# Sandwich layer on one core: inner tiles of the feed-forward block turned by DMA exchange and VectorE, weight parts and final norms moved to ScalarE, new orders

## What is computed

```python
x = x + _layernorm(attention(_layernorm(x), w_qkv, w_dense))      # causal, softmax over keys
x = x + _layernorm(ffn(_layernorm(x), w1, s1, w3, s3, w2, s2))
# ffn: every linear first quantises its input per row and block of 128 columns (amax / 448 + 1e-12)
g = linear_dsv3(xf, w1, w1_scale); u = linear_dsv3(xf, w3, w3_scale)
y = linear_dsv3(silu(g) * u, w2, w2_scale)
```

## Time and profile before

| | before |
|---|---|
| median of 3 runs | 1162.52 us |
| the profiled execution, its own time | 1162.25 us |
| its span, first to last instruction | 1160.4 us |
| TensorE busy | 1136.9 us (98%), 5618 matmuls and transposes |
| VectorE busy | 841.9 us (73%) |
| GpSimd busy | 743.9 us (64%) |
| ScalarE busy | 605.6 us (52%) |
| mean granted TensorE clock | 0.997 |

### The profile page before, as it was taken

How to read it: one execution, slowest core, us unless ns; L and a number is a source line. 1 busy time by engine, 2 the same in 40 slices (tenths; PEclk the granted TensorE clock), 3 DMA queues, 4 the chain that set the end, 5 groups by cost and what they waited for, 6 DMA issues and landing times. The chain is left out here.

```text
span 1160.4 us, 17601 instructions
## 1 busy us (share of the span) xinstructions
PE 1136.9 (98%) x5618; PEld 953.6 (82%) x5618; DVE 841.9 (73%) x1935; ACT 605.6 (52%) x1300; POOL 743.9 (64%) x829
## 2 busy tenths in 40 slices
PE   9999999999999999999999999999999999999996
PEld 7888888888888888888888888888887788888884
DVE  5545445458898897988888988988668955666568
ACT  6532324247766676767667676766578621111111
POOL 7844456435864955956838649558855767677636
PEclk9999999999999999999999999999999999999998
DMA  6443454326476585484574765754220011110101
GB/s 220 136 167 151 186 206 189 146 91 205 126 222 206 162 258 178 136 284 137 190 246 130 228 205 160 252 184 157 90 73 2 1 55 55 56 49 5 54 0 72
DMA packets 122098, 164.45 MB, mean 142 GB/s; under 512 B 10400, under 2 KB 95904, under 8 KB 118688
## 3 DMA queue, kind: packets, MB, share of 16 engines
q1 hardware_dynamic: 122016, 163.44, 42.8%
HBM read 98.78 MB, written 64.62 MB: 141 GB/s over the span
## 5 line engine op out<-in xcount | busy, mean ns | idle before, releaser
L816 POOL TENSOR_SCALAR probs_long<-probs_long,rsum 128x896 f32<-128x896 f32 (+9 forms) x124 | 118.0, 954 | 69.3 <-DVE rsum L1285 68.9
L1070 ACT ACTIVATE probs_long<-probs_long,negmax 128x896 f32<-128x896 f32 (+9 forms) x124 | 121.5, 980 | 70.5 <-DVE negmax L1279 69.7
L816 POOL TENSOR_SCALAR probs_short<-probs_short,rsum 128x416 f32<-128x416 f32 (+15 forms) x128 | 85.1, 669 | 112.9 <-DVE rsum L1285 112.2
L1520 PE MATMUL psS<-kT_hi,qT_hi 128*128 128x256 f32 (+8 forms) x384 | 134.7, 351 | 0.3
L1520 PE MATMUL psS<-kT_lo,qT_hi 128*128 128x256 f32 (+8 forms) x384 | 128.3, 334 | 0.0
L1520 PE MATMUL psS<-kT_hi,qT_lo 128*128 128x256 f32 (+8 forms) x384 | 128.3, 334 | 0.0
L1664 PE MATMUL psOY<-wd_hi,oT_hi 128*128 128x512 f32 x256 | 107.2, 419 | 2.0 <-DVE oT_lo L1214 1.2
L757 POOL TENSOR_TENSOR qT_lo<-q_raw,qT_hi 128x512 fp32r<-128x512 f32 x64 | 86.6, 1357 | 33.4 <-ACT qT_hi L1054 31.0
L1664 PE MATMUL psOY<-wd_hi,oT_lo 128*128 128x512 f32 x256 | 100.7, 393 | 0.0
L1664 PE MATMUL psOY<-wd_lo,oT_hi 128*128 128x512 f32 x256 | 100.4, 392 | 0.0
L1649 PE MATMUL psOY<-pT_hi,v_hi 128*128 128x512 f32 x222 | 92.5, 417 | 4.2 <-DVE pT_lo L1214 4.2
(11 more groups left out here) (185 smaller groups left out, 3293.4 us busy)
## 6 DMA issues: line engine op xcount, KB each, us to landing
q_raw<-q_scr SPq DMA_DIRECT2D x64, 256.0 KB, 3.5
p_scr<-probs_long SPq DMA_DIRECT2D x24, 512.0 KB, 3.2
probs_long<-p_scr SPq DMA_DIRECT2D x96, 128.0 KB, 3.5
raw<-in_w_qk SPq DMA_DIRECT2D x10, 1024.0 KB, 5.6
p_scr<-probs_long SPq DMA_DIRECT2D x21, 448.0 KB, 3.0
probs_long<-p_scr SPq DMA_DIRECT2D x84, 112.0 KB, 3.0
q_scr<-cB SPq DMA_DIRECT2D x16, 512.0 KB, 2.6
q_scr<-cA SPq DMA_DIRECT2D x16, 512.0 KB, 2.9
```

Of the source, the lines that this page charges most:

```text
L816: nc.gpsimd.tensor_scalar(row, row, rsum[:, column(t, h)], 1.0, ALU.mult, ALU.mult).then_inc(p_ready, 1)
L1070: nc.scalar.activation(row, row, ACT.Exp, bias=negmax[:, column(t, h)], scale=-1.0, accum_out=lsum[:, column(t, h)]).then_inc(e_done, 1)
L1520: last = nc.tensor.matmul(dst, a, b, start=(start and k == 0), stop=(stop and k == len(terms) - 1), skip_group_check=resumed)
```

## The change

In words:

- Inner tiles 0 to 52 are no longer turned by TensorE. GpSimd writes the scaled tile into a ring of four (`hidden`), SyncE stores it to DRAM (`hidden_away(n)`), then fetches tile n-1 with its 32-row blocks exchanged in four DMAs of 32 KB (`hidden_back(n-1)`), and VectorE turns the blocks (`turn_hidden`). High and low part are made from SBUF instead of PSUM. Tiles 53, 54, 55 (LAST_TURNS = 3) stay with TensorE (`turn_last`).
- The down product runs four tiles behind gate and up instead of two (LAG = 4). So the list of chunk 0 has four "DN" items instead of six, and four stand behind the last gate and up product instead of two.
- High parts of the weights of chunks 2 to 6 are copied by ScalarE (`hi_of_piece`); GpSimd takes the low part one step later (`low_of_piece`). Loads of up and down weights are separate, the up weights' one placed in step 5 of a chunk between a store and the fetch behind it.
- The last norms, for seven of the eight row tiles, are made of a sum that comes with the last addition, a square with its sum and the normalisation on ScalarE, and root and offset on GpSimd (`finish`, `square_last`, `norm_last`, `add_last`).
- `swap_back` in attention fetches 14 of 16 blocks (the two outer corners stay where they are).
- The tables that shift the items are replaced for all engines, attention included.

The diff, cut:

```diff
-    ATTENTION += [("X", 1), ("GU", 0), *[("Y", T - 1, h) for h in range(HG)], ("A", T - 1), ("X", 2), ("GU", 1), ("TH", 0)]
+    ATTENTION += [("X", 1), ("GU", 0), *[("Y", T - 1, h) for h in range(HG)], ("A", T - 1), ("X", 2), ("GU", 1)]
     for n in range(2, NT):
-        ATTENTION += [("X", n + 1)] * (n + 1 < NT) + [("GU", n), ("DN", n - 2), ("TH", n - 1)]
+        ATTENTION += [("X", n + 1)] * (n + 1 < NT) + [("GU", n)]
+        if n >= LAG:
+            ATTENTION.append(("DN", n - LAG))
+        if n >= LAG - 1:
+            ATTENTION += [("TT", n - LAG + 1), ("TH", n - LAG + 1)]
...
+            def hidden_away(n, m):
+                sp.wait_ge(h_ready, n + 1)
+                sp.dma_start(h_scr[m % RING], hidden[:, m % RING, :]).then_inc(h_out[m % 2], 16)
+            def hidden_back(m, stored):
+                slot = m % RING
+                sp.wait_ge(h_out[m % 2], stored)
+                for c in range(HG):
+                    sp.dma_start(hidden[c * SPAN:(c + 1) * SPAN, slot, :].rearrange("q (a x) -> q a x", a=HG),
+                                 h_scr[slot, :, c * CW // HG:(c + 1) * CW // HG].rearrange("(a q) x -> q a x", a=HG)
+                                 ).then_inc(h_in[slot], 16)
...
+                for m in range(2 * NT):
+                    hidden_away((2 * NT) * r + NT + m, NT + m)
+                    if m % NT == KT + 1:
+                        load_up(2 * r + 3 + m // NT)
+                    if m % NT == NT - 1:
+                        load_down(2 * r + 3 + m // NT)
+                    hidden_back(NT + m - 1, (16 * NT) * r + 16 * ((NT + m - 1) // 2 + 1))
...
                 for i in range(NT):
-                    quantise_hidden(c * NT + i, i % 2)
+                    quantise_hidden(c * NT + i, (0 if slot == 0 else NT) + i)
...
-                            prepare(c + 1, 1 - slot, i)
-                    elif i >= 2:
-                        finish(i - 2)
+                            scale_piece(c + 1, i)
+                        if 1 <= i <= PIECES:
+                            low_of_piece(c + 1, 1 - slot, i - 1)
+                    elif i >= LAG:
+                        finish(i - LAG)
+                        if i > LAG:
+                            add_last(i - LAG - 1)
...
+            def feed_forward_step(n, m, loads, last=-1):
+                turn_hidden(n - LAG + 1, m - LAG + 1, loads)
                 make_hidden(n, m % 2)
-                lo_of_hidden(n - 1, (m - 1) % 2)
-                add_down(n - 2, (m - 2) % NT)
+                lo_of_hidden(n - LAG + 1, m - LAG + 1)
+                if last >= 0:
+                    finish(n - LAG, last)
+                else:
+                    add_down(n - LAG, (m - LAG) % NT)
...
+            for n in range((C - 2) * NT, C * NT):
+                silu_gate(n, n % 2)
+                if 1 <= n - (C - 2) * NT <= PIECES:
+                    hi_of_piece(C - 1, 0, n - (C - 2) * NT - 1)
+                s = n - LAG - 1 - (C - 1) * NT
+                if s >= 0:
+                    square_last(s)
+                hi_of_hidden(n - LAG + 1, n - LAG + 1)
+                if s >= 1:
+                    norm_last(s - 1)
...
+            def step(n, m):
+                parity = (m // NT) % 2
+                gate_up(n, m % 2, LAST[m % NT], up_w[parity])
+                if isinstance(n, int) and C * NT - LAST_TURNS <= n - 1 < C * NT - 2:
+                    turn_last(n - 1, (n - 1) % 2)
+                down(n - LAG, m - LAG, parity if m % NT >= LAG else 1 - parity)
```

Of the tables, one entry each shows the form:

```diff
-                ("P", 7, 1, 0): -9.1, ("PV", 7, 4): -4.4, ("S", 7, 0): -0.6, ("S", 7, 2): 4.4, ("Y", 7, 1): 4,
+                 ("P", 57, 1, 3): 1.1, ("RQ", 57): -4.6, ("E", 58, 2): 20.4, ("P", 58, 0, 0): -23.4, ("P", 58, 0, 1): -4.4,
```

More of the change, by code:

```diff
@@ L1509, in _ @@
-            for s in (NT - 2, NT - 1):
-                add_down((C - 1) * NT + s, s)
-                finish(s)
-            finish(NT)
+                n = (C - 2) * NT + m
+                feed_forward_step(n, n, 16 * HG * ((n - LAG + 1) // RING + 1), last=m - LAG - NT)
+            lo_of_last(C * NT - 3, 1)
+            for s in range(NT - LAG, NT):
+                n = (C - 1) * NT + s
+                if n + 2 < C * NT:
+                    lo_of_last(n + 2, n % 2)
+                finish(n, s)
@@ L1515, in _ @@
+            tile = y[:, LAST[NT - 1], :]
+            dve.wait_ge(rstd_fin, 1)
+            link(normalise(tile, tile, mv, rstd, NT - 1))
+            nc.vector.tensor_tensor(x1[:, LAST[NT - 1], :], x1[:, LAST[NT - 1], :], tile, ALU.add).then_inc(last_ready, 1)
         @block.tensor
```

280 lines of the change are left out of this document (203 added, 77 removed), and 193 rows, old and new, of tables (ACT_LATER, ACT_NORMS, DVE_LATER, DVE_NORMS).

## The result

The changed kernel takes 1146.31 us (median of 4 runs, 1145.94 to 1147.73), the kernel before 1162.65 us beside it (4 runs, 1162.3 to 1163.21): ratio 0.9861, 95% interval 0.9844 to 0.9878. Faster by 16.3, or 1.4%, which is clear of the spread of the runs.

The account below looks back on a forecast made before the run. The prediction took TensorE to bound the kernel in three stages. Loop -10.6, chunk 0 -0.5, end +2.3 and attention -1.0 summed to -9.8, so 1152.7 us, with a range of 1147 to 1157.5.

Parts of the forecast that it names:

- part 5: Attention: `swap_back` moving an eighth less brings nothing; the new tables bring -1 us, with ends -5 and +3.
- Rival C: Better orders pay in chunk 0, attention and the end: all three 1145.9, two of three 1147; chance 0.20.
- parts 1 and 2: Loop: without the turn a step falls from 4.334 to 4.10, -10.6 us; the other engines and the exchange keep 4.10.
- A: Loop: the exchange becomes the bound; at a landing of 3.5 the step is 4.37, +12.7, so 1165.4; chance 0.05.
- B: Loop: VectorE and GpSimd hold each other up, steps about 4.25; with slower chunk 0 1159.2; chance 0.12.
- E: Loop: transposes were hidden under weight loads, so the gain is nil and the end +2.3: 1165; chance 0.02.
- part 3: Chunk 0: the two down products that left are mostly idle time here; -0.5 us, between +1.5 and -3.
- part 4: End: four down products instead of two, GpSimd holding the key; 18.1 instead of 15.85, +2.3 us, between 0 and +4.

Follow-up runs that it names:

- the filled run: Changed kernel with 49 transposes of a constant, read by nobody, on TensorE in five waits of chunk 0: 1147.35 us (0.9874).
- the altered end: Changed kernel with tile 55 scaled ahead of an addition and the additions of row tiles 4, 5 and 6 on VectorE: 1145.11 us (0.9854).

## Why the prediction was wrong, point by point

**Attention (part 5) failed.** The step read: "TensorE's idle time bounds the gain at 5.5 plus what each stop costs in pipelining, some 8 in all ... I take -1, ... with -5 and +3 as ends." The bound was nearly right (9.1 was measured: 1.44 in each of 6.3 groups, of which 0.7 at the wait, 0.2 and 0.3 at two places that no list of waits names, the rest in smaller ones). What failed is that I took -1 from a bound of -8, and cut the end at -5 with no row that said so; the runs gave -9.1, nearly all of it by the new orders, which keep VectorE's low parts and GpSimd's subtraction apart. Rival C had the mechanism, at 0.20 and with 4 in attention; against it stood "that the rows show no single wait that a new table would take away". They did: eight waits of the same kind, at one place of each group, and a group of operations that lasted longer for 768 columns than for 896 (1343 against 1121 ns). One look at the two engines around one such stop would have shown the collision. Had attention stood at -8 or -9, all else kept, the forecast would have been near 1145, about 1 below the measurement, by chunk 0's error.

**The loop (parts 1 and 2) was right**, -10.8 against -10.6, with some luck in the 0.2. A typical step is 4.08, not 4.10: it loses the turn's 0.22 and a little of its slots; the stops give most of that back, and they differ between executions: the loop is 194.8 to 197.0 long in the profiles of kernels that share its edits and its fetches. VectorE is busy 118.5 of 190, 2.5 of each step, less than my 3.0 to 3.3. The low part from two SBUF tiles costs 0.43 (0.42 from PSUM), the transpose 0.44, where 0.34 stood. Rivals A, B and E did not come. VectorE waits for the exchange in 26 steps, where I had it once a chunk; mostly harmless, since the low part is wanted a step later, but behind loads of weights it reaches TensorE (0.9 us in all here, 1.9 in the filled run's two stops).

**Chunk 0 (part 3) had the wrong sign**, +1.4 against -0.5, inside its bounds of +1.5 and -3. Its own working came to 938.4 against 938.25, that is +0.15, and the -0.5 had no row. The step that failed is that the last normalised tile would be turned when it was before. Behind the start of the first gate and up product that turn came at 32.3 before and comes at 33.1 now, 0.8 later; from the turn to step 8 it is 9.6 in place of 9.1, where the working had 9.4. I followed VectorE's list and not GpSimd's, though the chain of the kernel before runs through GpSimd there:

```profile
920.05 1.30 POOL up_lo L757
```

That this is the cause is not shown.

**The end (part 4) was right** in its number, 18.1, and by the named chain up to GpSimd's last root. Behind it I had GpSimd's additions last. In the trace they end at 1140.95 and VectorE's normalisation and addition, which my sum did not have, at 1141.49. What came before took 0.8 less than added up; this 0.5 and a last store of 2.6 in place of 2.4 make that good. That the sum fits to a tenth is luck.

## What to carry to other kernels

Where an engine stops for the same operation at the same place of every period, look at what the other engines run beside that operation before you call the gain of a new order unknowable; an operation whose mean is longer than that of a larger tile is a sign. A bound read from the trace is a term with its end at the bound; a smaller value needs a row of its own. When a wait is taken away, price the next item in the same queues as well, and where TensorE stands still for a microsecond or two several times in a row, read the granted clock before comparing two versions.

## What the runs showed of the hardware

- VectorE's and GpSimd's operations that read two SBUF tiles nearly take turns: 0.94 and 1.29 alone, 1.98 and 2.00 when they meet. Operations that read one tile are held as well: VectorE's scale of 128x2 takes 0.17, but 1.13 in one step beside GpSimd's subtraction, its four scalings of 128x128 take 1.1, 2.3 or 3.4, GpSimd's scaling of 128x640 takes 0.80 alone and 1.58 beside a low part, and its pass over 128x512 0.62 alone and 1.32 and 1.21 beside low parts.
- SyncE's issue of a DMA takes 0.43 to 0.47 whether it moves 32 or 16 KB, and a fetch lands after 1.9 or 1.8; nine take 4.23, more than a step of 4.08, and fill the queue.
- TensorE's granted clock fell to its lower level for some microseconds of chunk 0 in seven of ten profiles of kernels with the changed chunk 0 and unfilled waits, one of the changed kernel itself among them, behind stops of 1 to 2.5 us. It stayed at 1.00 in all five profiles with the waits filled by transposes at 0.11. Chunk 0 took 44.7 to 45.1 in six of the seven (42.7 in the altered end's), and 42.6 to 43.4 in the five.
- What spreads the changed kernel's runs from 1145.65 to 1150.02 is only in part that clock: with the waits filled, and a mean clock of 0.998, one execution still took 1149.51. Two other sources are seen in profiles, VectorE's four scalings (about 0.7 of chunk 0) and late fetches in the loop (up to 1.9); what made 1149.51 has no profile and stays open.
